# Two packed images out of one PSUM sum: one 32-bit integer pass in place of a rounding pass and a subtraction

## The chip, the cores and the metric

The kernel runs on one core of a Trainium2 chip. A core has five engines that run beside each other and meet at semaphores: TensorE (PE in the profile), VectorE (DVE), ScalarE (ACT), GpSimd (POOL) and SyncE (SP, which here only starts transfers). The metric is the device time of the whole kernel in microseconds. Before the change it was 318.55 us, the median of three runs (317.15 to 320.28).

## The reference, cut to what matters

A batch of 32 images with 64 channels of 28 x 28 passes through two blocks. The first one is the binary convolution block that the change touches:

```
xr  = tile(_gn(x), (1, 4, 1, 1))                   # 4 groups, all with the same input
out = conv3x3(sign(xr), sign(w1), groups=4)        # integers
out = relu(batchnorm(out, bn1))
out = conv3x3(sign(out), sign(w2), groups=4)       # sign of a relu: 0 or 1, "the gate"
out = batchnorm(out, bn2) * lambdas
out = sum over the 4 groups
x   = x + relu(out + _gn(x))
```

The second block multiplies the normalised x by a resized mask, computes a 7 x 7 attention convolution over three planes, multiplies by its sigmoid, normalises, scales, applies a relu and adds the result to x. In both blocks `_gn` is a normalisation over pairs of channels.

Because both convolutions take signs or gates, their sums are small integers. That allows two images to be computed in one sum: one image's value is multiplied by a large factor, the other's is added, and the two are taken apart afterwards.

## The kernel before

**Tiles.** The 32 images make 16 tiles (`NT`) of two images. A tile is 128 partitions (2 images x 64 channels) by 784 pixels. Tile t goes through the first block in iteration k = t of a software pipeline of 15 turns (k = 1 to 15, with a head for tile 0 and a tail), and through the steps of the second block in the iterations after it.

**First convolution.** `join` (L857) adds 2046 (`IMG`) times the first image's signs to the second image's signs, `pack_signs` (L439) copies the result to `E`, and `conv1` (L871) computes, for each of two halves q of the output channels, 784 sums of the form 2046*a + b. They lie in PSUM (`big`, in slots shared with other sums). ACT's `round_sums1` (L449) takes them out in two passes: L452 divides by 2046 and adds a large constant, which rounds to a, and L457 takes the constant away again and writes a as 16-bit floats in `first`. DVE's `gates` (L610) then has three instructions for each q: L612 compares a with a threshold and writes 1024 or 0 to `gate0`, L614 computes b = sum - 2046*a in PSUM, and L618 compares b, adds `gate0` and writes the packed gates to `S2`.

**Second convolution.** `conv2` (L884) runs over the two halves hh of the image rows, `round_sums2` (L459) and `move_back` (L467) on ACT and `split_sums` (L623) on DVE take the two images' sums apart into `RD`, `mix` (L898) sums the groups with weights `wa`, and `finish_block` (L630) on DVE adds the normalised x.

**Order.** Each engine has one instruction stream, written out by hand, and nothing is reordered. In turn k it is:

- PE: `conv1(k,0)`, `group_2(k-2)`, `conv1(k,1)`, `mix(k-1)`, `join(k+1)`, three `turn(k-2)`, `conv2(k,0)`, `conv2(k,1)`, and for odd k an `attention`.
- ACT: word or round of `c2(k-1,1)`, its move to `RD`, `sign_x(k+1)`, `round_sums1(k,0)`, `normalise2(k-2)`, `round_sums1(k,1)`, `relu_block(k-1)`, `pack_signs(k+1)`, `last_relu(k-5)`, the same for `c2(k,0)`, and for odd k a `sigmoid`.
- DVE: `split_sums(k-1,1)`, `terms2(k-2)` (four one-column instructions, L580 to L585), `stats_o(k-5)`, `gates(k,0)`, `finish_block(k-1)`, `gates(k,1)`, three `reduce_chunks(k-2)` (L651, L653), `stats_x(k+5)`, `split_sums(k,0)`, `stats_x1(k-1)`.
- POOL: `power2(k-2)`, `mask_column(k-2)`, `make_u(k-2)` (L349, 784 columns), `scale3(k-5)` (five one-column instructions, L374 to L382), `add_x(k-1)` (L367), `attend(k-4)` (L362), `last_sum(k-5)` (L387).

`turn(k-2,2)` on PE waits for the first of the three `reduce_chunks`, and stands ahead of `conv2(k,0)`. `group_2(k-2)` on PE waits for `stats_x1(k-2)` on DVE. `finish_block(k-1)` waits for `mix(k-1)`.

## Time and profile before

| | |
|---|---|
| median of the runs | 318.55 us (317.15 to 320.28) |
| span of the profiled execution, first to last instruction | 313.7 us |
| mean granted TensorE clock | 0.917 |
| PE busy | 239.8 us, 76% |
| DVE busy | 233.7 us, 74% |
| ACT busy | 184.0 us, 59% |
| POOL busy | 159.5 us, 51% |
| DMA | 28.86 MB, mean 92 GB/s |

The profiled execution's own time is not given apart from its span. The span leaves out what lies around the first and the last instruction: 318.55 - 313.7 = 4.85 us by the median.

A row of the timeline reads: start in us from the span's start, duration in us, engine, line, operation, what is written <- what is read, count, and in brackets the engine's idle time before it with what ended it. A row of the groups reads: line, engine, operation, tiles, shape and type, count | busy us in total, mean ns of one | idle us of the engine before them. In this profile the duration of one instruction overlaps the start of the next one on its engine by a little under 0.1 us when nothing separates them.

### The profile page before, as it was taken

The page shows a single profiled execution, that of the slowest core. Times are in us where ns is not written, and L with a number is a line of the kernel's source. Part 1 is how long each engine was busy: PE and PEld are TensorE (multiplying, and loading weights), DVE is VectorE, ACT ScalarE, POOL GpSimd, SP SyncE. Part 2 cuts the span into 40 slices and gives each one's busy share as a digit, 9 for nine tenths or more (in the row PEclk, how much of TensorE's full clock was granted, in tenths as well). Part 3 has the DMA queues.
Part 4 walks back from the last instruction along what each step waited for, and adds up shares of the span by engine and source line. Part 5 has one row for each costly group of instructions (what it writes and reads, how often), then busy time and mean ns, then how long its engine had stood idle before and what let it go on. Part 6 is the DMA issues. An engine that isn't in the chain of part 4 may idle for free.

```text
span 313.7 us, 7083 instructions
## 1 busy us (share of the span) xinstructions
PE 239.8 (76%) x2742; PEld 152.2 (49%) x2742; DVE 233.7 (74%) x554; ACT 184.0 (59%) x223; POOL 159.5 (51%) x215
## 2 busy tenths in 40 slices
PE   7294798687888778888887697969696969676860
PEld 3252555345554445445554464546454645454550
DVE  3338754769886896979998969899968687758373
ACT  3434252384858584848486848675876768544221
POOL 3200410222423456576747656774768475938763
PEclk9858677699999999979999999999999999979885
DMA  7980000523015402631253314211611141131113
GB/s 202 310 270 3 0 2 0 155 65 106 2 54 135 124 27 78 174 95 64 86 155 101 104 58 131 80 51 55 154 54 53 74 137 53 53 117 38 51 53 154
DMA packets 11946, 28.86 MB, mean 92 GB/s; under 512 B 2285, under 2 KB 3565, under 8 KB 11757
## 3 DMA queue, kind: packets, MB, share of 16 engines
q1 hardware_dynamic: 11481, 28.13, 29.2%
q8 instruction: 22, 0.36, 0.5%
q10 hardware_dynamic: 432, 0.29, 0.4%
q14 instruction: 11, 0.09, 0.1%
HBM read 21.79 MB, written 6.61 MB: 91 GB/s over the span
## 4 chain that ended last, share of the span: by engine, by line
PE 31%; DVE 28%; issue 17%; ACT 15%; DMA 3%; POOL 3%; SPq 0%; ACTq 0%; DVEq 0%; POOLq 0%
PE big L892 15%; DVE big L614 9%; ACT round L465 5%; PE small L938 5%; ACT first L457 3%; DVE bnst L556 3%; DMA X<-in_x 3%; PE small L927 3%; ACT round L452 3%; ACT signs L437 3%; DVE gate L612 3%; DVE red L651 2%; DVE RD L627 2%; DVE S L618 2%; PE big L878 2%
## 5 line engine op out<-in xcount | busy, mean ns | idle before, releaser
L892 PE MATMUL big<-S,w2t 64*64 64x392 f16 x1152 | 59.3, 361 | 7.5 <-DVE S L618 7.5
L465 ACT ACTIVATE round<-big 128x784 f16<-128x784 f32 x32 | 26.1, 815 | 54.7 <-PE big L892 54.7
L878 PE MATMUL big<-E,w1t 64*128 64x392 f16 x576 | 55.8, 337 | 0.0
L927 PE MATMUL small<-cs,o 128*112 128x130 f32 x224 | 32.9, 287 | 27.2 <-DVE red L653 24.1
L627 DVE SCALAR_TENSOR_TENSOR RD<-round,big 128x784 f16<-128x784 f16 x32 | 30.7, 960 | 25.6 <-ACT round L465 25.6
L892 PEld LDWEIGHTS big<-S,w2t 64*64 64x64 f16 x1152 | 34.9, 115 | 27.1 <-DVE S L618 4.3
L927 PEld LDWEIGHTS small<-cs,o 128*112 128x112 f32 x224 | 26.4, 176 | 35.3 <-DVE red L653 27.4
L349 POOL TENSOR_TENSOR o<-o,mask_b 128x784 f32<-128x784 f32 x16 | 29.5, 1845 | 21.9 <-ACT o L484 21.9
L909 PE MATMUL big<-RD,wa 128*64 128x392 f16 x384 | 38.2, 352 | 1.3 <-DVE RD L627 1.3
L341 POOL TENSOR_TENSOR r<-ve,mhalf 128x1 f32<-128x1 f32 x16 | 8.9, 559 | 56.0 <-DVE ve L585 56.0
L556 DVE BATCH_NORM_STATS2 bnst<-X 128x6 f32<-128x392 f32 x64 | 32.8, 554 | 5.3 <-DMA X<-in_x 5.3
L878 PEld LDWEIGHTS big<-E,w1t 64*128 64x128 f16 x576 | 25.9, 95 | 21.1 <-issue 5.0
L367 POOL TENSOR_TENSOR X<-X,acc 128x784 f32<-128x784 f32 x15 | 27.7, 1843 | 15.4 <-ACT acc L478 15.4
L618 DVE SCALAR_TENSOR_TENSOR S<-big,thr,gate 128x784 f16<-128x784 f32 x32 | 33.2, 1038 | 1.1
L614 DVE SCALAR_TENSOR_TENSOR big<-first,big 128x784 f32<-128x784 f16 x32 | 31.1, 972 | 0.0
L909 PEld LDWEIGHTS big<-RD,wa 128*64 128x64 bf16 x384 | 21.7, 116 | 16.1 <-issue 4.7
L452 ACT ACTIVATE round<-big 128x784 f32<-128x784 f32 x32 | 25.7, 804 | 5.9 <-PE big L878 5.8
L472 ACT ACTIVATE RD<-round 128x784 f16<-128x784 f16 x32 | 27.4, 857 | 1.0
L457 ACT ACTIVATE first<-round 128x784 f16<-128x784 f32 x32 | 27.4, 857 | 1.0
L478 ACT ACTIVATE acc<-acc,b 128x784 f32<-128x784 f32 x16 | 15.2, 948 | 20.4 <-DVE acc L635 20.4
L362 POOL TENSOR_TENSOR o<-o,att_b 128x784 f32<-128x784 f32 x14 | 25.9, 1852 | 0.0
L651 DVE TENSOR_REDUCE red<-small 112x6 f32<-112x384 f32 (+1 forms) x48 | 22.0, 463 | 4.6 <-PE small L927 4.1
(119 smaller groups left out, 355.5 us busy)
## 6 DMA issues: line engine op xcount, KB each, us to landing
X<-in_x SPq DMA_DIRECT2D x16, 392.0 KB, 6.4
mask_b<-mask_rows SPq DMA_DIRECT2D x32, 196.0 KB, 3.5
out<-o SPq DMA_DIRECT2D x16, 392.0 KB, 2.3
att_b<-attention_rows SPq DMA_DIRECT2D x28, 196.0 KB, 3.9
o<-in_w SPq DMA_DIRECT2D x3, 576.0 KB, 9.7
o<-in_masks SPq DMA_DIRECT2D x1, 512.0 KB, 11.0
cs<-in_cst SPq DMA_DIRECT2D x1, 385.0 KB, 11.1
o<-in_sel SPq DMA_DIRECT2D x1, 343.0 KB
```

The costliest lines, as they stand in the source:

```text
L349: pool.tensor_tensor(o[:, t, :], o[:, t, :], mask_b[:, t % 2, :], ALU.mult).then_inc(u_ready, 1)
L452: act.activation(round1[:, :], sums(f"c1_{q}"), ACT.Copy, bias=ROUND, scale=1.0 / IMG)\
L457: act.activation(first[:, q, :], round1[:, :], ACT.Copy, bias=-ROUND).then_inc(whole1, 1)
L465: act.activation(round2[:, hh, :], sums(f"c2_{hh}"), ACT.Copy, bias=BASE - MID).then_inc(rounded2, 1)
L556: dve.bn_stats(bnst[:, n, t, i, :], src[:, HALF * i:HALF * (i + 1)]).then_inc(stats[n], 1)
L614: dve.scalar_tensor_tensor(sums(f"c1_{q}"), first[:, q, :], -IMG, sums(f"c1_{q}"), ALU.mult, ALU.add)\
L618: dve.scalar_tensor_tensor(inside(S2[:, t % 2, q, :]), sums(f"c1_{q}").rearrange("p (h w) -> p h w", w=W), thr[:, q:q + 1], gate0[:, q, :] ...
L627: dve.scalar_tensor_tensor(RD[:, t % 2, hh, 1, :], round2[:, hh, :], BASE, sums(f"c2_{hh}"), ALU.subtract, ALU.subtract).then_inc(split, 1)
L878: mm = pe.matmul(acc[:, LOW + HALF * hh:LOW + HALF * (hh + 1)], w1t[64 * hh:64 * hh + 64, s, q * P:(q + 1) * P], window(RH * hh, s // 3, s ...
L892: mm = pe.matmul(acc[64 * q:64 * q + 64, LOW + HALF * r:LOW + HALF * (r + 1)], w2t[64 * r:64 * r + 64, s, 64 * q:64 * q + 64], window(RH * ...
L909: mm = pe.matmul(big[SLOT["y"]][64 * i:64 * i + 64, at:at + HALF], wa[:, i, r, n, :], RD[:, t % 2, hh, i, HALF * r:HALF * (r + 1)], start= ...
L927: mm = pe.matmul(small[1 - n % 2][0:CP, at:at + P + 2], o[:, t, CP * j:CP * (j + 1)], cs[:, K_ID:K_ID + P + 2], start=True, stop=True)
```

## The change

For the first convolution ACT makes one pass over each packed sum. It multiplies by 65536/2046, adds 32768 and writes a 32-bit integer (`word1`). The upper 16 bits of that integer are a and the lower 16 bits are proportional to b plus an offset. DVE reads both through 16-bit views of the same memory (`high1`, `low1`), in which neighbouring elements are four bytes apart. The second pass of ACT (L457) and DVE's subtraction in PSUM (L614) are gone. The last gate instruction reads `low1` from SBUF where it read PSUM, and a second threshold `thr_low` in the new scale is computed once in the head.

For the second convolution ACT writes `word2` in 32 bits. The first image's value is copied from `high2` by ACT, with as many passes as before. `split_sums` becomes a one-input instruction on `low2` where it was a two-input one on `round2` and PSUM. `wa` loses its factor -1024.

Two waits move: `join(t)` and `conv1(t,1)` on PE wait for ACT's integer pass, where they waited for DVE's gates and split.

```diff
-        round1 = sb("round1", [P, HW], F32)
-        first = sb("first", [P, 2, HW], F16)
-        round2 = sb("round2", [P, 2, HW], F16)
+        word1 = sb("word1", [P, 2, HW], I32)
+        word2 = sb("word2", [P, 2, HW], I32)
...
+        low1, high1 = (word1[:, :, :].bitcast(dt).rearrange("p q (n two) -> p q n two", two=2)[:, :, :, h]
+                       for h, dt in ((0, U16), (1, I16)))
...
-            def round_sums1(t, q):
+            def words1(t, q):
                 act.wait_ge(conv1_done, t * 2 + q + 1)
-                wait(act, whole1, t * 2 + q)
-                act.activation(round1[:, :], sums(f"c1_{q}"), ACT.Copy, bias=ROUND, scale=1.0 / IMG)\
-                   .then_inc(rounded1, 1)
-                act.wait_ge(rounded1, t * 2 + q + 1)
-                wait(act, parted1, t * 2 + q - 1)
-                wait(act, gated0, t * 2 + q - 1)
-                act.activation(first[:, q, :], round1[:, :], ACT.Copy, bias=-ROUND).then_inc(whole1, 1)
+                wait(act, gated, t * 2 + q - 1)
+                act.activation(word1[:, q, :], sums(f"c1_{q}"), ACT.Copy, bias=WORD / 2, scale=WORD / IMG)\
+                   .then_inc(worded1, 1)
...
-                act.activation(round2[:, hh, :], sums(f"c2_{hh}"), ACT.Copy, bias=BASE - MID).then_inc(rounded2, 1)
+                act.activation(word2[:, hh, :], sums(f"c2_{hh}"), ACT.Copy, bias=LIFT, scale=WORD)\
+                   .then_inc(worded2, 1)
...
-                act.activation(RD[:, t % 2, hh, 0, :], round2[:, hh, :], ACT.Copy, bias=-BASE).then_inc(whole2, 1)
+                act.activation(RD[:, t % 2, hh, 0, :], high2[:, hh, :], ACT.Copy).then_inc(whole2, 1)
...
             def gates(t, q):
-                dve.wait_ge(whole1, t * 2 + q + 1)
-                dve.tensor_scalar(gate0[:, q, :], first[:, q, :], thr[:, q:q + 1], GATE, ALU.is_gt, ALU.mult)\
+                dve.wait_ge(worded1, t * 2 + q + 1)
+                dve.tensor_scalar(gate0[:, q, :], high1[:, q, :], thr[:, q:q + 1], GATE, ALU.is_gt, ALU.mult)\
                    .then_inc(gated0, 1)
-                dve.scalar_tensor_tensor(sums(f"c1_{q}"), first[:, q, :], -IMG, sums(f"c1_{q}"), ALU.mult, ALU.add)\
-                   .then_inc(parted1, 1)
-                dve.wait_ge(parted1, t * 2 + q + 1)
+                if t == 0:
+                    dve.wait_ge(thr_ready, 1)
+                dve.wait_ge(gated0, t * 2 + q + 1)
                 wait(dve, conv2_done, t * 2 - 2)
                 dve.scalar_tensor_tensor(inside(S2[:, t % 2, q, :]),
-                                         sums(f"c1_{q}").rearrange("p (h w) -> p h w", w=W), thr[:, q:q + 1],
+                                         low1[:, q, :].rearrange("p (h w) -> p h w", w=W), thr_low[:, q:q + 1],
                                          gate0[:, q, :].rearrange("p (h w) -> p h w", w=W), ALU.is_gt, ALU.add)\
                    .then_inc(gated, 1)
...
-                    dve.scalar_tensor_tensor(RD[:, t % 2, hh, 1, :], round2[:, hh, :], BASE, sums(f"c2_{hh}"),
-                                             ALU.subtract, ALU.subtract).then_inc(split, 1)
+                    dve.tensor_scalar(RD[:, t % 2, hh, 1, :], low2[:, hh, :], LIFT, 1.0 / UNIT,
+                                      ALU.subtract, ALU.mult).then_inc(split, 1)
...
-                wait(pe, gated, 2 * t - 1)
+                wait(pe, worded1, 2 * t - 1)
...
-                    wait(pe, split, 2 * t - 1)
+                    wait(pe, worded2, 2 * t - 1)
```

DVE's stream in an iteration of the loop before, from the second `gates` over the three `reduce_chunks` and `stats_x` to `split_sums(k,0)`; the names behind the arrow are what is read (`first` is a, `big` is PSUM):

```order
L614 SCALAR_TENSOR_TENSOR big<-first,big 128x784
L618 SCALAR_TENSOR_TENSOR S<-big,thr,gate 128x28x28 [waits conv2_done,parted1]
L651 TENSOR_REDUCE red<-small 112x3x2 [waits att_done,turned]
...
L558 BN_AGGR mv<-bnst 128x2 [waits stats0]
L627 SCALAR_TENSOR_TENSOR RD<-round,big 128x784 [waits y_done,rounded2]
```

The same place after the change, where `word` is one of the two integer tiles in SBUF:

```order
L619 TENSOR_SCALAR gate<-word,thr 128x784 [waits worded1]
L625 SCALAR_TENSOR_TENSOR S<-word,thr_low,gate 128x28x28 [waits conv2_done,gated0]
L658 TENSOR_REDUCE red<-small 112x3x2 [waits att_done,turned]
...
L565 BN_AGGR mv<-bnst 128x2 [waits stats0]
L634 TENSOR_SCALAR RD<-word 128x784 [waits y_done,worded2]
```

Nothing has changed its place; the 784-column subtraction is out, the gate instruction reads two tiles of SBUF and no PSUM, and the split reads one tile of SBUF. ACT's stream in an iteration before, from the move of `c2(k-1,1)` to the first convolution's second half:

```order
L472 ACTIVATE RD<-round 128x784 [waits y_done,rounded2]
L437 ACTIVATE signs<-X,nm 128x784 [waits joined,mean1]
L452 ACTIVATE round<-big 128x784 [waits whole1,conv1_done]
L457 ACTIVATE first<-round 128x784 [waits gated0,parted1,rounded1]
L484 ACTIVATE o<-X,nmr,r 128x784 [waits shift2]
L452 ACTIVATE round<-big 128x784 [waits whole1,conv1_done]
L457 ACTIVATE first<-round 128x784 [waits gated0,parted1,rounded1]
```

and after it:

```order
L479 ACTIVATE RD<-word 128x784 [waits y_done,worded2]
L447 ACTIVATE signs<-X,nm 128x784 [waits joined,mean1]
L462 ACTIVATE word<-big 128x784 [waits gated,conv1_done]
L491 ACTIVATE o<-X,nmr,r 128x784 [waits shift2]
L462 ACTIVATE word<-big 128x784 [waits gated,conv1_done]
```

Two of the seven rows are out, so `normalise2` (`o<-X,nmr,r`) stands right behind the first integer pass.

## Rows read from the trace of the kernel before

**Rows 1.** The page: the span, and busy time by engine (us, share of the span).
```profile
span 313.7 us, 7083 instructions
...
PE 239.8 (76%) x2742; PEld 152.2 (49%) x2742; DVE 233.7 (74%) x554; ACT 184.0 (59%) x223; POOL 159.5 (51%) x215
```

**Rows 2.** Instruction groups (shapes apart): total us, mean ns | idle before.
```profile
L614 DVE SCALAR_TENSOR_TENSOR big<-first,big 128x784 f32<-128x784 f16 x32 | 31.1, 972 | 0.0
...
L618 DVE SCALAR_TENSOR_TENSOR S<-big,thr,gate 128x784 f16<-128x784 f32 x32 | 33.2, 1038 | 1.1
...
L627 DVE SCALAR_TENSOR_TENSOR RD<-round,big 128x784 f16<-128x784 f16 x32 | 30.7, 960 | 25.6 <-ACT round L465 25.6
...
L612 DVE TENSOR_SCALAR gate<-first,thr 128x784 f16<-128x784 f16 x32 | 13.4, 419 | 14.0 <-ACT first L457 13.9
...
L457 ACT ACTIVATE first<-round 128x784 f16<-128x784 f32 x32 | 27.4, 857 | 1.0
...
L580 DVE TENSOR_SCALAR nm<-small 128x1 f32<-128x1 f32 x18 | 2.8, 155 | 1.6 <-PE small L845 0.8 <-PE small L854 0.7
```

**Rows 3.** Timeline, tile 8 to 9: start us, us, engine line op, tiles, [idle before].
```profile
168.81 0.82 ACT L465 ACTIVATE round<-big 128x784 f16<-128x784 f32 x1 [2.44 <-PE big L892]
...
171.75 0.93 DVE L627 SCALAR_TENSOR_TENSOR RD<-round,big 128x784 f16<-128x784 f16 x1
...
171.88 0.38 PE L854 MATMUL small<-mv,cs 128*128 128x2 f32 x2
...
172.87 0.80 ACT L452 ACTIVATE round<-big 128x784 f32<-128x784 f32 x1
...
173.83 2.18 PE L909 MATMUL big<-RD,wa 128*64 128x392 f16 x24
...
174.59 0.43 DVE L612 TENSOR_SCALAR gate<-first,thr 128x784 f16<-128x784 f16 x1 [0.28 <-ACT first L457]
...
175.57 1.84 POOL L349 TENSOR_TENSOR o<-o,mask_b 128x784 f32<-128x784 f32 x1 [1.38 <-ACT o L484]
...
176.89 1.02 DVE L635 SCALAR_TENSOR_TENSOR acc<-X,r,big 128x784 f32<-128x784 f32 x1
...
177.83 0.42 DVE L612 TENSOR_SCALAR gate<-first,thr 128x784 f16<-128x784 f16 x1
...
180.12 0.55 DVE L651 TENSOR_REDUCE red<-small 112x6 f32<-112x384 f32 x1
...
182.97 0.82 ACT L465 ACTIVATE round<-big 128x784 f16<-128x784 f32 x1 [2.44 <-PE big L892]
...
182.99 1.85 POOL L387 TENSOR_TENSOR o<-o,X 128x784 f32<-128x784 f32 x1
```

**Rows 4.** Timeline, tile 9 to 10, a stretch with an attention.
```profile
186.48 0.80 ACT L465 ACTIVATE round<-big 128x784 f16<-128x784 f32 x1
...
190.64 0.42 DVE L612 TENSOR_SCALAR gate<-first,thr 128x784 f16<-128x784 f16 x1 [0.64 <-ACT first L457]
...
191.62 1.84 POOL L349 TENSOR_TENSOR o<-o,mask_b 128x784 f32<-128x784 f32 x1 [1.75 <-ACT o L484]
...
196.16 0.55 DVE L651 TENSOR_REDUCE red<-small 112x6 f32<-112x384 f32 x1
```

**Rows 5.** Timeline at two places where DVE and POOL overlap.
```profile
152.79 1.85 POOL L387 TENSOR_TENSOR o<-o,X 128x784 f32<-128x784 f32 x1
...
152.88 1.78 DVE L608 TENSOR_SCALAR b<-nmr,beta 128x4 f32<-128x4 f32 x1
...
285.02 1.85 POOL L362 TENSOR_TENSOR o<-o,att_b 128x784 f32<-128x784 f32 x1
...
285.55 2.15 DVE L641 TENSOR_TENSOR X<-X,acc 128x784 f32<-128x784 f32 x1
...
286.82 2.57 POOL L387 TENSOR_TENSOR o<-o,X 128x784 f32<-128x784 f32 x1
```

**Rows 6.** Timeline, the first gates of the program.
```profile
24.64 0.42 DVE L612 TENSOR_SCALAR gate<-first,thr 128x784 f16<-128x784 f16 x1 [4.03 <-ACT first L457]
```

49 lines of the change are left out of this document (29 added, 20 removed).

## The prediction

> **What bounds the kernel now.** I read the page first, then the groups of instructions, then the timeline of two stretches of the loop. The page shows no full engine: PE is busy for 76% and DVE for 74% of the span [rows 1]. So the bound is a loop through several engines. The timeline of one turn, from the first L465 of tile 8 to that of tile 9, takes 182.97 - 168.81 = 14.16 us [rows 3]. I call its start T. ACT takes the sums out (L465, two halves), makes the next signs, and rounds conv1's first half (L452, L457). DVE had waited only 0.28 us when the first gate instruction L612 started at T+5.78. Three gate instructions bring it to `finish_block` at T+8.08 (L635), and three more, from 177.83 on, to the first `reduce_chunks` at 180.12: that is 2.29 us for one `gates`. PE's last `turn` waits for that reduce, and `conv2` stands behind it, so the next T follows 182.97 - 180.12 = 2.85 us after the reduce. PE does not bind the first half of the turn: `mix` had ended at 173.83 + 2.18 = 176.01, 0.88 us before `finish_block` began. A turn with an attention (T to T longer by PE's attention work) has the same chain behind its second L465 at 186.48, there with 0.64 us of waiting for L457 [rows 4]. Both `gates` of a turn lie on the chain, and that makes DVE's subtraction L614 (972 ns, 32 times, no idle time before it) the heaviest thing that the change removes [rows 2].
>
> **What the change removes and adds.**
>
> *The gates.* Out: L614. The last instruction of `gates` keeps its operation; I give it its present 1.04 us [rows 2]. All 784-column instructions of DVE with two inputs lie within 0.96 to 1.04 us whether they read PSUM twice or once, so I see no gain from leaving PSUM. The first one, L612, costs 0.42 us now on dense 16-bit data; in the new kernel its input stands in every second 16-bit place. Bounds: 0.42 below, and above the full-rate 0.96 of L627 [rows 2]. One column costs 0.155 us (L580), so the 784 dense columns take 0.26 us more than one. If only one value comes with each 4-byte word, that part doubles: 0.155 + 0.53 = 0.69 us. I take 0.69. A `gates` then lasts 0.69 + 0.04 (the second waits for the first) + 0.95 (1.04 less the overlap with the next instruction) = 1.68 us, which is 0.61 less than 2.29.
>
> *ACT.* The second pass L457 goes (0.86 us, 32 times) [rows 2]. The one pass writes 4 bytes as L452 did, so it stays at 0.80. Bounds of the integer output and of the copy from every second place: nothing, and the 0.06 between 0.80 and 0.86 us. ACT has 41% of the span idle [rows 1], which hides that.
>
> *The splits.* One input in place of two; the same 0.69 instead of 0.96: 0.27 us less each, bounds 0.42 and 0.96.
>
> *Without anything in the way* the first `gates` of a turn could start about 0.9 us earlier, and then `finish_block` meets a new bound: it cannot start before `mix` has ended, 176.01 + 0.07 = 176.08, in place of 176.89. So 0.81 us are won before it and 0.61 behind it, 1.42 us per turn.
>
> *The port.* Two places of the trace say that this is not what will happen. L641, a DVE instruction with two inputs in SBUF, began 0.53 us after POOL's L362, lasted 2.15 us, and POOL's next instruction L387, which started with DVE waiting, lasted 2.57 us instead of 1.85 [rows 5]. DVE waited for POOL to end, then POOL waited for DVE. L608, a one-input instruction of four columns with input and output in SBUF, lasted 1.78 us and ended with POOL's L387 at 154.66 [rows 5]; one column of such an operation costs 0.155 us. By these rows a DVE instruction with two SBUF inputs, or one SBUF input and an SBUF output in this fast form, and a POOL instruction exclude each other, and who comes first keeps the way to his end. Before the change only L612 was of that kind, and it sat in gaps of POOL. Now all six big instructions of a turn are: two L612, two last gates, two splits; against POOL's four 1.84 us instructions.
>
> The Trainium skill says the same in *SBUF — State Buffer*, section "Who interferes with whom": VectorE and GpSimd share a port pair that is locked for a whole instruction, by VectorE instructions with two SBUF inputs and by copies and tensor_scalar in the two-port modes. It speaks against this change: without that rule the sum would be 1.42 us per turn, with it what follows.
>
> *A turn with an attention* [rows 4]. L612 starts 0.64 us earlier, at 190.00; the last gate runs from 190.73 to 191.77. `make_u` (L349, 191.62 before) is wanted about 0.7 us earlier, at 190.9, since the removed L457 stood before its ACT source; it is blocked until 191.77 and ends 1.84 later, at 193.61. The second L612 would be wanted 0.94 after `finish_block`, near 193.0, and waits for 193.61. The reduce comes at 193.61 + 1.68 = 195.29 instead of 196.16: 0.87 us won.
>
> *A turn without an attention* [rows 3]. The end of `make_u` again starts the second gates, so the next T comes 1.68 + 2.85 = 4.53 us after that end, and `make_u` starts 6.37 before T. `last_sum` (L387) follows the start of `make_u` by 182.99 - 175.57 = 7.42 us, so it starts at T+1.05, or up to 1.2 later if DVE holds up POOL's small instructions (0.69 + 1.04, less what overlaps). The first split is wanted at T+0.86 and waits until T+1.05 or T+2.25, where the instruction before `last_sum` ends. The second one (T+2.94 before) then waits for the end of `last_sum`, near T+3.5 or T+4.75. From there 0.61 (the split, less overlap) and 1.72 (what stood between L627 at 171.75 and L612 at 174.59, less L627's own 0.84 and the 0.28 idle) lead to the first gates, at T+5.8 or T+7.1. PE's `group_2` (L854, T+3.07) is held only in the second case, by 1.05. Then 0.73 + 1.04 for the gates, 1.84 for `make_u` behind them and 4.53 to the next T: 14.0 or 15.2 us, against 14.16. I take the middle, 0.43 us lost.
>
> *Head and tail.* The first gates waited 4.03 us for ACT [rows 6]; they start 0.86 earlier, and both `gates` of tile 0 are 0.61 shorter: 2.08 us. Tile 1 gives 0.61. The tail gives one split, 0.27. In the turns from tile 1 to 2 and 2 to 3 POOL has neither `attend` nor `last_sum` yet; there only the wait for `make_u` is left, some 1.1 us won each.
>
> *Sum*: -2.08 - 0.61 - 2 x 1.1 - 6 x 0.87 + 6 x 0.43 - 0.27 = -7.8 us. Of the profiled execution's span of 313.7 us that leaves 305.9; with the 4.85 us by which the median lies above that span, 310.7. I say 310.5.
>
> **The rivals.**
>
> *A, the port does not matter.* DVE and POOL fall beside each other, or the new forms do not need the shared way. Then 14 turns at 1.42 and 2.96 from head, tile 1 and tail: -22.8 us, 295.7. For it: L612 and POOL lived side by side for the whole loop. Against it: rows 5.
>
> *B, reading every second place runs at full rate* (0.96 us) and then needs no port in the one-input forms. A `gates` saves 0.34, the splits nothing, and only the last gate meets `make_u`. An attention turn then wins about 0.8, another between 1.1 won and 0.7 lost: 305 to 313.
>
> *C, slower: `make_u` overtakes the first gates.* In my timetable the last gate instruction of the first half starts at 190.73 and `make_u` is wanted at 190.9. Once the first gate instruction takes over 0.2 us longer than I say, or POOL comes that much earlier, POOL goes first and the last gate waits 1.84 us. `finish_block` stands behind it on DVE, and PE behind that. An attention turn then costs 0.15 more than before, another one about 1.3 more, and the first two win nothing: -2.96 + 6 x 0.15 + 6 x 1.3 = +5.7 us, 324.3.
>
> *D, the change does nothing.* Each turn without attention loses what the other wins (15.2 us each, +1.05 instead of +0.43): 310.7 + 6 x 0.62 = 314.4, near the edge.
>
> **How the numbers follow.** 1% of 318.55 is 3.2 us, about what a measurement of this kernel can tell from no change; faster means under 315.4. My forecast with D as its upper end (304 to 318) 0.52; A 0.20; B 0.15; C 0.13. Faster: all of A, nearly all of B, and about 0.4 of the 0.52, 0.73. Same: the rest of the forecast and a little of B and C, 0.15. Slower: 0.12. The range takes A's value at its lower end and stops short of C: 296 to 320; the forecast's own range is 304 to 318.
>
> **What would show each step right or wrong.** The first gate instruction at 0.69 us where POOL is idle, the last at 1.04, the split at 0.69. The price of the port: maxima near 2 to 3 us in these three groups, starts of POOL's L349 at the end of a gate, and POOL's 1.84 us instructions and its one-column ones getting longer. Attention turns shorter by about 0.9 us and the others unchanged. If the three groups all show a median equal to their minimum, A is right. If `finish_block` starts right behind `mix` in every turn, PE has become the bound. If the last gate of the first half regularly lasts near 2.9 us, C is right. The forecast is wrong above all if POOL's phase in the turn is another than I worked out, since each of its four big instructions is longer than any gap I reasoned with.

## The result and the profile after the change

The changed kernel takes 302.33 us (median of 298.91 to 304.31) against 318.41 us for the kernel before on the same chip; the ratio is 0.9445 with a 95% interval of 0.9385 to 0.9505. The medians are of all executions; every ratio and interval here is taken from those alone that ran undisturbed, since some executions take about a per cent longer at a lower granted clock, and so 0.9445 isn't 302.33/318.41. A second measurement beside later experiments gave 300.9 us, ratio 0.9475 (0.9425 to 0.9526). So the change wins 16 to 18 us. I had forecast 8, and a range of 296 to 320: the sign was right, the time lay inside the range, and the size was half of what came. The profiled execution has a span of 297.1 us beside 313.7 before.

The page after the change, its span and its busy times (before: [rows 1]):

```profile
span 297.1 us, 6991 instructions
...
PE 238.0 (80%) x2742; PEld 152.4 (51%) x2742; DVE 216.5 (73%) x523; ACT 159.2 (54%) x191; POOL 182.9 (62%) x215
```

DVE is busy 17 us less, ACT 25 us less, and POOL is busy 23 us *more*, although it has the same 215 instructions. The groups show why (line engine, tiles, count | busy us, mean ns | idle before; before: [rows 2]):

```profile
L634 DVE TENSOR_SCALAR RD<-word 128x784 f16<-128x784 uint16 x32 | 33.1, 1035 | 22.2 <-ACT word L471 22.2
...
L625 DVE SCALAR_TENSOR_TENSOR S<-word,thr_low,gate 128x784 f16<-128x784 uint16 x32 | 34.7, 1084 | 1.3
...
L619 DVE TENSOR_SCALAR gate<-word,thr 128x784 f16<-128x784 int16 x32 | 22.8, 712 | 6.1 <-ACT word L462 6.1
...
L359 POOL TENSOR_TENSOR o<-o,mask_b 128x784 f32<-128x784 f32 x16 | 35.6, 2226 | 15.4 <-ACT o L491 15.4
...
L397 POOL TENSOR_TENSOR o<-o,X 128x784 f32<-128x784 f32 x13 | 28.3, 2180 | 0.0
...
L386 POOL TENSOR_TENSOR r<-ve,mhalf 128x1 f32<-128x1 f32 x16 | 18.3, 1141 | 1.3
```

`make_u` (L359) has a mean of 2226 ns and `last_sum` (L397) of 2180 where POOL's instructions of this size took 1.84 and 1.85 us before [rows 3], and the one-column power L386 doubled to 1141 ns. The DVE split L634 has a mean of 1035 ns. The means hide two populations; the split and the gate by line (duration min/median/max):

```profile
L619 DVE TENSOR_SCALAR gate<-word,thr x32: 574/627/1280, 22.2 to 251.0; 128x784 f16<-128x784 int16 x32
```
```profile
L625 DVE SCALAR_TENSOR_TENSOR S<-word,thr_low,gate x32: 1036/1040/2497, 23.0 to 252.1; 128x784 f16<-128x784 uint16 x32
```
```profile
L634 DVE TENSOR_SCALAR RD<-word x32: 514/571/1894, 36.7 to 260.3; 128x784 f16<-128x784 uint16 x32
```

Free of POOL, the strided gate instruction takes 0.574 to 0.63 us and the split 0.51 to 0.57; the last gate takes the 1.04 us it took from PSUM. The maxima are waits for POOL.

The timeline of a turn without attention (start, us, engine line, tiles, [idle before]; before: [rows 3]):

```profile
155.77 0.82 ACT L471 ACTIVATE word<-big 128x784 int32<-128x784 f32 x1 [0.24 <-PE big L901]
156.24 1.85 POOL L372 TENSOR_TENSOR o<-o,att_b 128x784 f32<-128x784 f32 x1
...
156.62 1.89 DVE L634 TENSOR_SCALAR RD<-word 128x784 f16<-128x784 uint16 x1 [0.98 <-ACT word L471]
...
158.06 2.16 POOL L397 TENSOR_TENSOR o<-o,X 128x784 f32<-128x784 f32 x1
...
159.62 1.02 DVE L634 TENSOR_SCALAR RD<-word 128x784 f16<-128x784 uint16 x1
...
162.20 0.58 DVE L619 TENSOR_SCALAR gate<-word,thr 128x784 f16<-128x784 int16 x1
162.81 1.04 DVE L625 SCALAR_TENSOR_TENSOR S<-word,thr_low,gate 128x784 f16<-128x784 uint16 x1
...
163.17 2.38 POOL L359 TENSOR_TENSOR o<-o,mask_b 128x784 f32<-128x784 f32 x1 [1.01 <-ACT o L491]
...
164.88 1.09 DVE L619 TENSOR_SCALAR gate<-word,thr 128x784 f16<-128x784 int16 x1
...
169.82 0.83 ACT L471 ACTIVATE word<-big 128x784 int32<-128x784 f32 x1 [0.23 <-PE big L901]
```

The turn lasts 169.82 - 155.77 = 14.05 us, 0.11 less than the 14.16 before. The first split (156.62) waits for `attend` (L372), and `last_sum` (L397) then waits for the split; the second split (159.62) waits for `last_sum`; `make_u` (L359) starts 0.36 us behind the last gate L625, is held by it, and holds the second first-gate instruction (164.88) in turn. The next turn has an attention (before: [rows 4]):

```profile
173.33 0.80 ACT L471 ACTIVATE word<-big 128x784 int32<-128x784 f32 x1
...
177.37 1.04 DVE L625 SCALAR_TENSOR_TENSOR S<-word,thr_low,gate 128x784 f16<-128x784 uint16 x1
...
177.72 2.38 POOL L359 TENSOR_TENSOR o<-o,mask_b 128x784 f32<-128x784 f32 x1 [1.01 <-ACT o L491]
...
180.70 1.33 POOL L386 TENSOR_TENSOR r<-ve,mhalf 128x1 f32<-128x1 f32 x1
...
181.52 0.55 DVE L658 TENSOR_REDUCE red<-small 112x6 f32<-112x384 f32 x1
```

From the second L471 at 173.33 to the reduce at 181.52 it takes 8.19 us, against 196.16 - 186.48 = 9.68 before.

Lengths of the turns from tile to tile, measured from one first L465 (after: L471) to the next, in the profiled executions (us). The last four columns are experiments, told below; in "POOL cut" POOL's large instructions are shortened to 8 columns:

| turn | before | after | last gate from PSUM (e5) | first half only (e8) | before, POOL cut (e7) | after, POOL cut (e6) |
|---|---|---|---|---|---|---|
| 0 to 1 | 24.57 | 25.21 | 25.99 | 28.09 | 27.35 | 26.26 |
| 1 to 2 | 15.48 | 14.05 | 13.87 | 13.43 | 15.28 | 13.95 |
| 2 to 3 | 14.17 | 12.94 | 12.94 | 15.36 | 14.16 | 12.95 |
| 3 to 4, attention | 16.04 | 14.47 | 14.46 | 14.47 | 16.05 | 14.46 |
| 4 to 5 | 14.17 | 12.72 | 12.62 | 13.05 | 14.16 | 12.63 |
| 5 to 6, attention | 17.26 | 14.57 | 14.46 | 14.56 | 17.48 | 14.46 |
| 6 to 7 | 14.51 | 14.32 | 13.05 | 14.41 | 14.35 | 12.95 |
| 7 to 8, attention | 16.05 | 14.57 | 14.62 | 14.57 | 16.04 | 14.46 |
| 8 to 9 | 14.16 | 14.05 | 12.63 | 13.04 | 14.17 | 12.63 |
| 9 to 10, attention | 16.05 | 14.56 | 14.45 | 14.56 | 16.05 | 14.46 |
| 10 to 11 | 14.35 | 14.34 | 13.06 | 15.30 | 14.35 | 12.95 |
| 14 to 15 | 13.77 | 14.04 | 12.62 | 13.04 | 13.88 | 12.63 |

The gain of the change is in the turns with an attention, 1.5 us each, and in the early ones. The turns without attention from tile 6 to tile 13 win 0.0 to 0.2 us, and the one from tile 14 to 15 loses 0.27.

One length is the same in all these profiles: the next turn starts 2.85 or 2.86 us after the first `reduce_chunks` of the turn, as long as TensorE's granted clock stays at 1.00 (2.4 GHz). Where it fell to 0.50 (1.2 GHz) behind an idle time of PE, it took 3.54 to 4.45 us. In the kernel before that happened once, from tile 5 to 6 (4.07 us), and in the changed one never between tile 1 and tile 15. So 1.2 of the 2.7 us won in that turn belong to the clock in this one profile, and not to the chain.

### The profile page after: what moved, and what is told of

Same layout as the page of the kernel before. It is cut to its first block, busy times and chain, and to the rows that moved or that the text cites. A ratio compares the mean times of both kernels' runs of the same rounds, so it can differ in the third digit from the quotient of the medians.

```text
span 297.1 us, 6991 instructions
## 1 busy us (share of the span) xinstructions
PE 238.0 (80%) x2742; PEld 152.4 (51%) x2742; DVE 216.5 (73%) x523; ACT 159.2 (54%) x191; POOL 182.9 (62%) x215
## 4 chain that ended last, share of the span: by engine, by line
PE 56%; DVE 23%; issue 11%; DMA 3%; ACT 3%; POOL 3%; SPq 1%; POOLq 0%; DVEq 0%; ACTq 0%
PE big L901 16%; PE big L887 13%; PE big L918 10%; DVE gate L619 5%; PE small L947 5%; PE small L936 4%; DVE RD L634 4%; DVE bnst L563 4%; DMA X<-in_x 3%; DVE S L625 2%; PE small L991 2%; ACT word L471 2%; DVE red L658 2%; PE small L863 1%; POOL o L359 1%
## 5 line engine op out<-in xcount | busy, mean ns | idle before, releaser
L936 PE MATMUL small<-cs,o 128*112 128x130 f32 x224 | 35.1, 303 | 26.6 <-POOL o L359 19.3
L634 DVE TENSOR_SCALAR RD<-word 128x784 f16<-128x784 uint16 x32 | 33.1, 1035 | 22.2 <-ACT word L471 22.2
L936 PEld LDWEIGHTS small<-cs,o 128*112 128x112 f32 x224 | 28.8, 190 | 35.7 <-POOL o L359 25.2
L359 POOL TENSOR_TENSOR o<-o,mask_b 128x784 f32<-128x784 f32 x16 | 35.6, 2226 | 15.4 <-ACT o L491 15.4
L471 ACT ACTIVATE word<-big 128x784 int32<-128x784 f32 x32 | 26.1, 815 | 27.1 <-PE big L901 27.1
L377 POOL TENSOR_TENSOR X<-X,acc 128x784 f32<-128x784 f32 x15 | 29.3, 1957 | 13.9 <-ACT acc L485 13.9
L625 DVE SCALAR_TENSOR_TENSOR S<-word,thr_low,gate 128x784 f16<-128x784 uint16 x32 | 34.7, 1084 | 1.3
L507 ACT ACTIVATE o<-o,bi,sc 128x784 f32<-128x784 f32 x16 | 16.7, 1042 | 33.4 <-POOL sc L392 33.4
L485 ACT ACTIVATE acc<-acc,b 128x784 f32<-128x784 f32 x16 | 15.2, 949 | 26.8 <-DVE acc L642 26.8
L462 ACT ACTIVATE word<-big 128x784 int32<-128x784 f32 x32 | 25.8, 806 | 6.5 <-PE big L887 6.3
L397 POOL TENSOR_TENSOR o<-o,X 128x784 f32<-128x784 f32 x13 | 28.3, 2180 | 0.0
L918 PEld LDWEIGHTS big<-RD,wa 128*64 128x64 bf16 x384 | 20.8, 112 | 14.3 <-issue 4.7
L479 ACT ACTIVATE RD<-word 128x784 f16<-128x784 int16 x32 | 27.4, 857 | 1.0
L619 DVE TENSOR_SCALAR gate<-word,thr 128x784 f16<-128x784 int16 x32 | 22.8, 712 | 6.1 <-ACT word L462 6.1
```

Source lines behind the costliest of these rows:

```text
L359: pool.tensor_tensor(o[:, t, :], o[:, t, :], mask_b[:, t % 2, :], ALU.mult).then_inc(u_ready, 1)
L377: pool.tensor_tensor(X[:, t, :], X[:, t, :], acc0[:, t % 2, :], ALU.add).then_inc(x1_ready, 1)
L397: pool.tensor_tensor(o[:, t, :], o[:, t, :], X[:, t, :], ALU.add).then_inc(fin_added, 1)
L471: act.activation(word2[:, hh, :], sums(f"c2_{hh}"), ACT.Copy, bias=LIFT, scale=WORD)\
L619: dve.tensor_scalar(gate0[:, q, :], high1[:, q, :], thr[:, q:q + 1], GATE, ALU.is_gt, ALU.mult)\
L625: dve.scalar_tensor_tensor(inside(S2[:, t % 2, q, :]), low1[:, q, :].rearrange("p (h w) -> p h w", w=W), thr_low[:, q:q + 1], gate0[:, q, ...
```

## The experiments

The theory is that of the prediction: the changed kernel's chain is much shorter, and a part of what it wins is given back because DVE's and POOL's large instructions now exclude each other. The rivals are that the port costs nothing, and, for the gain itself, that ACT's second pass rather than DVE's subtraction carried it.

**e1 and e8, the first convolution's half alone.** The second convolution keeps its 16-bit tile and its split with one input in SBUF and one in PSUM.

```diff
-                act.activation(word2[:, hh, :], sums(f"c2_{hh}"), ACT.Copy, bias=LIFT, scale=WORD)\
+                act.activation(round2[:, hh, :], sums(f"c2_{hh}"), ACT.Copy, bias=BASE - MID)\
...
-                    dve.tensor_scalar(RD[:, t % 2, hh, 1, :], low2[:, hh, :], LIFT, 1.0 / UNIT,
-                                      ALU.subtract, ALU.mult).then_inc(split, 1)
+                    dve.scalar_tensor_tensor(RD[:, t % 2, hh, 1, :], round2[:, hh, :], BASE, sums(f"c2_{hh}"),
+                                             ALU.subtract, ALU.subtract).then_inc(split, 1)
```

> Only the first convolution's half of the change; the second convolution keeps its 16-bit tile and the split that reads SBUF and PSUM (0.96 us, no second SBUF operand). Port theory (a DVE instruction with two SBUF inputs, or in the fast one-input form, and a POOL instruction exclude each other): the first split of a turn no longer waits for POOL's attend (1.88 us in the changed kernel, 0.97 here), group_2 and mix on PE come about 0.9 us earlier, turns without attention are 0.5 to 0.9 us shorter, so 296 to 299 us. Rival (the port costs nothing, only busy time counts): the split is 0.39 us longer than the free 0.57, so 303 to 306 us.

> The first convolution's half alone once more, for a profile at full clock (the first one was taken at the low clock throughout). Port theory: the first split of a turn lasts 0.97 us and does not wait for POOL; group_2 is no longer held; turns without attention under 13.8 us, with attention near 14.6. If turns without attention stay at 14.0 to 14.3, the split was not what held them and another wait took its place.

Measured: e1 304.74 us, ratio 0.9576 (0.9493 to 0.9659), e8 303.47 us, ratio 0.9561 (0.9484 to 0.9637). Both totals lie in the range that I had given the rival (303 to 306 us), not in that of the port theory (296 to 299), so the totals alone speak against it. The profile of e1 was taken in an execution in which TensorE was granted 0.555 of its clock on average, near the low of its two levels (span 394.2 us); e8 exists for that reason. A turn without attention of e8:

```profile
162.45 0.82 ACT L471 ACTIVATE round<-big 128x784 f16<-128x784 f32 x1 [0.24 <-PE big L901]
162.90 1.86 POOL L372 TENSOR_TENSOR o<-o,att_b 128x784 f32<-128x784 f32 x1
...
163.30 0.97 DVE L634 SCALAR_TENSOR_TENSOR RD<-round,big 128x784 f16<-128x784 f16 x1 [0.98 <-ACT round L471]
...
167.87 0.57 DVE L619 TENSOR_SCALAR gate<-word,thr 128x784 f16<-128x784 int16 x1
...
175.49 0.82 ACT L471 ACTIVATE round<-big 128x784 f16<-128x784 f32 x1 [0.24 <-PE big L901]
```

The split (163.30) starts inside `attend` (162.90) and is not held, the first gates come 5.42 us after the turn's start instead of 6.43, and the turn lasts 13.04 us instead of 14.05. That part of the theory holds (0.97 us, under 13.8 us), and yet the whole kernel is not faster than the changed one. The table shows where it went: the turns 2 to 3 and 10 to 11 are 2.4 and 1.0 us longer. In the first of them POOL's `add_x` overtook the last gate:

```profile
85.65 2.13 POOL L377 TENSOR_TENSOR X<-X,acc 128x784 f32<-128x784 f32 x1
...
86.12 2.51 DVE L625 SCALAR_TENSOR_TENSOR S<-word,thr_low,gate 128x784 f16<-128x784 uint16 x1
```

`add_x` (L377) began 0.47 us before L625, which then lasted 2.51 us instead of 1.04. The other one, 10 to 11, has no such meeting. There PE was idle for 2.26 us behind `make_u`, its clock fell to 0.50, and the next turn came 3.76 us after the reduce instead of 2.86:

```profile
200.23 3.03 PE L936 MATMUL small<-cs,o 128*112 128x130 f32 x14 [2.26 <-POOL o L359]
203.19 3.63 PE L901 MATMUL big<-S,w2t 64*64 64x392 f16 x72
```

In the changed kernel the same 72 matmuls take 3.25 us. An idle time of PE of the same 2.26 us in the turn from 6 to 7 of e8 was followed by no fall of the clock; why one was and the other not stays open. From the start of tile 1's turn to that of tile 15, e8 takes 197.95 us, the changed kernel 197.81 and the same kernel in e9 197.11. What the split won in the late turns (1.0 us each in three of them) went into one meeting of the same two engines, one fall of the clock, and 0.1 to 0.3 us in each of two other turns. Most of the rest of the difference is the head (0 to 1, 28.09 against 25.21), but the changed kernel itself took 27.80 us there in e9, see the last section.

**e2, the second convolution's half alone.** The first one keeps ACT's two passes and the subtraction.

```diff
-                    dve.scalar_tensor_tensor(RD[:, t % 2, hh, 1, :], round2[:, hh, :], BASE, sums(f"c2_{hh}"),
-                                             ALU.subtract, ALU.subtract).then_inc(split, 1)
+                    dve.tensor_scalar(RD[:, t % 2, hh, 1, :], low2[:, hh, :], LIFT, 1.0 / UNIT,
+                                      ALU.subtract, ALU.mult).then_inc(split, 1)
```

> Only the second convolution's half; the first one keeps ACT's two passes and DVE's subtraction in PSUM. Port theory: the first split starts while POOL's last_sum runs and lasts near 1.5 us instead of 0.97, the second one 0.57; what one loses the other wins, 317 to 321 us. Rival (only busy time counts): both splits 0.39 us shorter, the 0.28 us of waiting before the first gates grow, 314 to 317 us.

Measured: 317.99 us, ratio 0.9932 (0.9862 to 1.0002); the turns are the old ones, 14.16 and 16.05. The first split starts inside POOL's `last_sum` and waits for it, the second one is free:

```profile
182.88 1.86 POOL L396 TENSOR_TENSOR o<-o,X 128x784 f32<-128x784 f32 x1
...
183.71 1.46 DVE L636 TENSOR_SCALAR RD<-word 128x784 f16<-128x784 uint16 x1 [0.98 <-ACT word L474]
...
187.19 0.57 DVE L636 TENSOR_SCALAR RD<-word 128x784 f16<-128x784 uint16 x1 [0.84 <-ACT word L474]
```

1.46 us against 0.97 before, then 0.57: the forecast "near 1.5, then 0.57" was met. The total can't tell the theory from its rival, since the interval reaches from 1.4% faster to no change; the turns and these two rows can. The second half of the change is worth nothing that I can tell from zero by itself.

**e3, ACT's second pass put back** into the changed kernel.

```diff
+                act.wait_ge(worded1, t * 2 + q + 1)
+                act.activation(first[:, q, :], high1[:, q, :], ACT.Copy).then_inc(whole1, 1)
...
-                dve.wait_ge(worded1, t * 2 + q + 1)
-                dve.tensor_scalar(gate0[:, q, :], high1[:, q, :], thr[:, q:q + 1], GATE, ALU.is_gt, ALU.mult)\
+                dve.wait_ge(whole1, t * 2 + q + 1)
+                dve.tensor_scalar(gate0[:, q, :], first[:, q, :], thr[:, q:q + 1], GATE, ALU.is_gt, ALU.mult)\
```

> The changed kernel with ACT's second pass put back (it copies the upper half to a dense 16-bit tile that the first gate instruction reads at 0.42 us). If ACT's pass was on the chain everywhere, 14 turns at 0.86 us and the head: 313 to 316 us. By the timeline of the changed kernel it is on the chain only in turns with an attention (the first gates wait there for ACT, elsewhere for DVE's own work): about +0.6 in each of six or seven of those turns, +0.7 in the head: 305 to 308 us.

Measured: 304.25 us, ratio 0.9575 (0.9465 to 0.9686). Attention turns take 14.93 us, 0.36 more than without the pass, and the other late ones 13.63 to 13.92, 0.4 *less*, because the gate instruction on the dense tile takes 0.37 to 0.43 us instead of 0.57. In an attention turn the first gates wait for ACT:

```profile
181.27 0.43 DVE L622 TENSOR_SCALAR gate<-first,thr 128x784 f16<-128x784 f16 x1 [0.64 <-ACT first L466]
```

I had expected +0.6 in an attention turn and 305 to 308 us, which was a little too much. So ACT's 27 us of second passes were worth the 1.9 to 3.4 us between 304.25 and the two medians of the changed kernel, and a part of that is one odd turn of 16.62 us (3 to 4) in which POOL held the last gate:

```profile
97.65 2.71 DVE L628 SCALAR_TENSOR_TENSOR S<-word,thr_low,gate 128x784 f16<-128x784 uint16 x1
97.69 1.84 POOL L378 TENSOR_TENSOR X<-X,acc 128x784 f32<-128x784 f32 x1 [0.29 <-ACT acc L488]
```

The gate's recorded start is 0.04 us ahead of POOL's, and it lost all the same, so recorded starts that close don't say who wins. The rival "ACT's pass carried the gain" (313 to 316) is out.

**e4, a DVE pass over PSUM put back** between the two gate instructions.

```diff
+                dve.scalar_tensor_tensor(sums(f"c1_{q}"), gate0_old[:, q, :], -IMG, sums(f"c1_{q}"), ALU.mult, ALU.add)\
+                   .then_inc(parted1, 1)
...
-                wait(pe, worded1, 2 * t - 1)
+                wait(pe, gated, 2 * t - 1)
```

> The changed kernel with a 784-column DVE instruction between SBUF and PSUM put back into each gates (0.97 us, its result unused), join waits for the gates again. If the subtraction was simply on the chain, +1.0 us at the second gates and part of that at the first: 302 + 14 x 1.0 to 1.6 = 316 to 325 us. If in addition POOL's make_u now starts before the last gate of the first half and holds it 1.84 us (rival C of the prediction), 325 to 335 us, and that instruction's median is near 2.5 us in the first half.

Measured: 365.82 us, ratio 1.1513 (1.1441 to 1.1584). That is 47 us slower than the kernel *before*, which has the same DVE passes and one more on ACT, and 31 us above the worst I had expected. The turns take 18.4 to 19.1 us. The profile shows what I had called rival C:

```profile
236.96 1.85 POOL L361 TENSOR_TENSOR o<-o,mask_b 128x784 f32<-128x784 f32 x1 [1.01 <-ACT o L493]
237.58 2.07 DVE L630 SCALAR_TENSOR_TENSOR S<-word,thr_low,gate 128x784 f16<-128x784 uint16 x1
...
241.65 1.84 POOL L379 TENSOR_TENSOR X<-X,acc 128x784 f32<-128x784 f32 x1
242.10 2.22 DVE L630 SCALAR_TENSOR_TENSOR S<-word,thr_low,gate 128x784 f16<-128x784 uint16 x1
...
244.91 0.78 PE L942 MATMUL small<-cs,o 128*112 128x130 f32 x2 [3.30 <-DVE red L665]
```

With 0.97 us more between the two gate instructions, POOL's `make_u` (236.96) starts 0.62 us ahead of the last gate (L630, 237.58), which lasts 2.07 us. In the second gates `add_x` (241.65) does the same, 2.22 us. Each turn thus pays 1.9 us for the two passes and 2.2 us for the two lost races, less some 1.3 us of waits for POOL that the changed kernel had and e4 has not: in the turn from 8 to 9 the reduce comes 13.99 us after the start instead of 11.19. A third part is the clock. PE stands idle for 3.30 us (244.91), and its granted clock is 0.50 from 245 to 248 us; the next turn starts 3.65 to 4.45 us after the reduce instead of 2.86. That happens in every one of the 14 turns and makes 18.2 of the 61.8 us by which this loop is longer (259.6 against 197.8 from tile 1 to 15). My 325 to 335 had one lost race per turn and no clock in it. So e4 shows the race, but it doesn't price the subtraction by itself. The margin by which the changed kernel wins that race is 0.36 us (162.81 to 163.17).

**e5, the last gate without a second SBUF operand.** It reads the packed sum from PSUM and so leaves out the right comparison of the second image.

```diff
-                                         low1[:, q, :].rearrange("p (h w) -> p h w", w=W), thr_low[:, q:q + 1],
+                                         sums(f"c1_{q}").rearrange("p (h w) -> p h w", w=W), thr_low[:, q:q + 1],
...
-                wait(pe, worded1, 2 * t - 1)
+                wait(pe, gated, 2 * t - 1)
```

> The changed kernel, but the last gate instruction reads the packed sum in PSUM instead of the lower half in SBUF, so that it has one SBUF tensor (join waits for the gates again, since PSUM is read longer). It leaves out the right comparison of the second image. Port theory: POOL's make_u lasts 1.85 instead of 2.38 us, POOL's one-column power in scale3 0.57 instead of 1.33, attend and last_sum end about 1.3 us earlier, the first split waits less in turns without attention (0.5 to 0.8 us each) and the second gates wait 0.15 less in the others: 294 to 299 us beside about 302 for the changed kernel. Rival (these waits are hidden): 301 to 303 us.

Measured: 293.23 us, ratio 0.9237 (0.9162 to 0.9311): 8 to 9 us under the changed kernel, and 0.8 under the range that I had given.

```profile
175.92 1.04 DVE L625 SCALAR_TENSOR_TENSOR S<-big,thr_low,gate 128x784 f16<-128x784 f32 x1
...
176.28 1.85 POOL L359 TENSOR_TENSOR o<-o,mask_b 128x784 f32<-128x784 f32 x1 [1.01 <-ACT o L491]
```
```profile
L625 DVE SCALAR_TENSOR_TENSOR S<-big,thr_low,gate x32: 1036/1037/1041, 23.8 to 246.2; 128x784 f16<-128x784 f32 x32
```

The instruction has the same 1.037 us with one operand in PSUM, but POOL's `make_u` beside it now takes 1.85 us, and no instance of L625 lasts longer than 1.041 us. The turns fall to 12.62 to 13.06 and 14.46 us.

**e6 and e7, POOL's large instructions cut to 8 columns** in the kernel after and before. Both leave out most of the mask and attention products and of two sums.

```diff
-                    pool.tensor_tensor(o[:, t, :], o[:, t, :], mask_b[:, t % 2, :], ALU.mult).then_inc(u_ready, 1)
+                    pool.tensor_tensor(o[:, t, 0:8], o[:, t, 0:8], mask_b[:, t % 2, 0:8], ALU.mult).then_inc(u_ready, 1)
```

> The changed kernel with POOL's four large instructions cut from 784 to 8 columns (it leaves out most of mask product, attention product and two sums); DVE's instructions then never wait for POOL. If the port takes gain away, this is well under the changed kernel by more than the next run is under the kernel before: 12.7 to 13.2 us per turn without attention and 14.4 with, 289 to 294 us. If the port costs nothing: 299 to 302 us.

> The kernel before with the same cut of POOL's instructions. In its turns POOL stands on no chain, so 14.2 and 16.05 us per turn stay and only the tail, where make_u, attend and the last sums are in series with other work, gets shorter by about 5 us: 311 to 314 us. The difference to the run with the changed kernel is what the change is worth without the port: 20 to 23 us if rival A of the prediction was priced right.

Measured: 287.23 us (ratio 0.9038, 0.8965 to 0.9111) and 314.57 us (0.9874, 0.9744 to 1.0004). Without POOL's large instructions the change is worth 27.3 us; with them it is 16.1 (302.33 against 318.41). From tile 1 on, the turns of e7 are those of the kernel before within 0.2 us, save two with a fall of TensorE's clock (17.48 from 5 to 6, 17.24 from 13 to 14), so POOL stood on no chain of the loop there. Both totals missed what I had expected, e6 by 1.8 us below and e7 by 0.6 above. From tile 1 on, the turns of e6 are those of e5 within 0.11 us, save one of 14.62 in e5. In the loop, from tile 1 to tile 15, the kernel before takes 212.3 us, the changed one 197.8, e5 190.3 and e6 190.1: the port costs the changed kernel 7.7 us there, and taking the last gate off it gives all but 0.2 back.

**e9, e10, e11 and e12, looking for a faster version.** e9 is the changed kernel once more. The other three try to sort the meetings by order. e10 is the first half alone with two edits:

```diff
                     pool.wait_ge(block_relu, t + 1)
+                    pool.wait_ge(gated, 2 * t + 4)
...
+                if k in (3, 7, 11):
+                    make_bias1(batch(k + 1))
                 gates(k, 0)
```

e11 is the whole change with the same edits; e12 is e10 with `make_bias1` moved behind `finish_block`:

```diff
                 finish_block(k - 1)
+                if k in (3, 7, 11):
+                    make_bias1(batch(k + 1))
```

> The changed kernel itself, beside the next two on one chip. If the times of its first measurement (298.9 to 304.3) are the spread of TensorE's granted clock in the head and tail, it stays at 299 to 304 us with the same turns of the loop (14.0 and 14.6 us).

> Only the first convolution's half of the change, and two orders changed: POOL's add_x waits until the last gate of its turn is done (in the profile of e8 it went first at 56.4 and 85.65 and held that gate for 1.46 us), and DVE makes the bias terms of the batches (L613, L615) before the first gates instead of behind the reduces (where L615 waited 1.6 us for POOL). Port theory: tile 1 and turns 2 to 3, 6 to 7 and 10 to 11 get 1.5 to 2.3 us shorter each: 296 to 299 us, faster than the changed kernel. Rival (these waits are hidden by other work): 303 to 305 us as in e1 and e8.

> The whole change with the same two orders. Tile 1 gets 1.46 us shorter and turn 10 to 11 about 0.3: 299 to 301 us. Turns without attention stay at 14.0 us since the first split still waits for attend.

> Only the first convolution's half of the change, POOL's add_x behind the last gate of its turn, and the bias terms of a batch between finish_block and the second gates instead of behind the reduces (e10 had them before the first gates, where they let POOL's make_u go first and hold the gate for 2.67 us). There the port is POOL's anyway. Port theory: no turn above 14.6 us, turns without attention 13.0 to 13.5 us, 293 to 298 us. Rival (the loop's waits only move): 300 to 304 us.

Measured: e9 300.9 us (0.9475), e10 306.51 us with executions scattered from 298.72 to 308.48, so that it decides nothing, e11 300.79 us (0.9504, 0.9458 to 0.955), e12 301.65 us (0.951, 0.9459 to 0.9561). None beats the changed kernel clearly. The totals of e9 and e11 are as expected; e10 was expected at 296 to 299 and e12 at 293 to 298, and both missed. The wait of `add_x` did in tile 1 what it should; the gate that lasted 2.50 us there has its 1.04 in e11, where POOL now comes behind:

```profile
51.91 2.12 POOL L377 TENSOR_TENSOR X<-X,acc 128x784 f32<-128x784 f32 x1 [10.79 <-ACT acc L485]
52.38 2.50 DVE L625 SCALAR_TENSOR_TENSOR S<-word,thr_low,gate 128x784 f16<-128x784 uint16 x1
```
```profile
52.51 1.04 DVE L626 SCALAR_TENSOR_TENSOR S<-word,thr_low,gate 128x784 f16<-128x784 uint16 x1
...
53.69 1.84 POOL L378 TENSOR_TENSOR X<-X,acc 128x784 f32<-128x784 f32 x1 [12.44 <-DVE S L626]
```

But turns 6 to 7 and 10 to 11 got longer, 15.86 and 15.57 us in e11 and 17.19 and 15.72 in e10. In e10, 0.3 us of bias terms ahead of the first gates were enough to let `make_u` go level with the last gate, in both turns:

```profile
139.19 0.23 DVE L616 TENSOR_SCALAR b<-nmr,beta 128x4 f32<-128x4 f32 x1
...
139.99 2.67 DVE L626 SCALAR_TENSOR_TENSOR S<-word,thr_low,gate 128x784 f16<-128x784 uint16 x1
139.99 1.84 POOL L359 TENSOR_TENSOR o<-o,mask_b 128x784 f32<-128x784 f32 x1 [1.01 <-ACT o L492]
```

In e11 no last gate is held (its longest is 1.043 us). There the clock is the larger part: PE was idle for 1.89 us before its `turn` matmuls, its clock fell to 0.50 in both turns, and the next turn came 4.05 and 3.62 us after the reduce instead of 2.86. Behind `finish_block` (e12) the same turns take 15.50 and 15.67 us, no last gate is held either, and the clock fell in both (3.54 and 3.73 us). The turn from 6 to 7 of e10 has such a fall too. I had not looked for this in the expectations. My expectation for e12, no turn above 14.6 us, failed, and I leave the best place for these small instructions open. The version that would be worth having is one with the timing of e5 and a right second comparison; I found no form of it.

## Why the prediction was right or wrong, point by point

**What bounds the kernel, and what the change removes: right.** With POOL out of the way (e7 to e6) an attention turn gets 1.59 us shorter and a late one without attention 1.3 to 1.5, and in e3 ACT's pass costs 0.36 us of an attention turn, net of what the dense gate instructions give back. e8 has the old split and the same 14.56 us in an attention turn, so the new split gives nothing there. What is left of the 1.5 us is DVE's subtraction and the two moved waits of PE; no run takes out the subtraction alone. Leaving PSUM made the last gate no faster (1.04 us). ACT's integer pass kept 0.80 us (L462 median 0.803), its strided copy 0.857.

**The port: right in kind.** First split behind `attend`, second behind `last_sum`, `make_u` behind the last gate, the second gates behind `make_u`: all four meetings are in the timeline of the changed kernel where the prediction put them, and e5, e6 and e7 show that removing them gives the time back. The trace agrees with what the Trainium skill states in *SBUF — State Buffer*, section "Who interferes with whom", on which instructions contend: the strided split and the last gate with two SBUF inputs are held, the one with an input in PSUM (e5) is not. The page says that the pair is locked for the whole instruction; how the recorded times look at its end comes next.

**The step that failed: the price of a turn with the port.** The attention turn was to win 0.87 us and won 1.48 to 1.57 (the one from tile 5 to 6 won 2.69, because it had taken 17.26 us before, in a stretch with a fall of TensorE's clock). The turn without attention was to lose 0.43 and won 0.0 to 0.2 from tile 6 to 13, lost 0.27 from 14 to 15, and won 1.45 from tile 4 to 5. Three parts of that error can be read from the rows. First, the strided one-input instruction takes 0.57 us where I had doubled the column part of L612 to 0.69; it runs free once on the path of each turn (162.20). Second, I let the waiting instruction start its full duration at the recorded end of the one that held the port. In the rows `make_u` ends 1.70 us after the gate that held it (163.17 + 2.38 against 162.81 + 1.04) where I had 1.84, and the gate instruction held by `make_u` ends 0.42 us after it (164.88 + 1.09 against 165.55), the held first split 0.42 us after `attend`, where I had 0.69. So a held instruction ends as if it had started some 0.15 us before the recorded end of its holder; whether the port is free that early or the held one has a start-up of its own that needs no port, no run here tells. My own [rows 5] had this already: L387 ended at 289.39, 1.69 us and not 1.85 behind the L641 that had held it (287.70), and the four-column L608, 0.23 us when free, ended 0.02 us behind L387. Third, these add up along the chain: in the turn without attention my second case had the first gates at T+7.1, the end of `make_u` at T+10.7 and the next T at 15.2; measured are T+6.43, T+9.78 and 14.05. POOL's phase was that of this second case, `attend` ending at T+2.3 (T+2.25 in the prediction). With the measured sizes the same timetable, worked through again after the result, gives T+6.43, T+9.78 and 14.04 for this turn, 0.12 us won, and 1.40 won for the attention turn. The sum is then -14.3 us instead of -7.8, or 304.3 us.

Two things in the loop stay outside that. The timetable put `last_sum` into all six turns, but in the one from tile 4 to 5 POOL has none yet and `attend` ends at T+0.75, before the split is wanted at T+0.86; so it is an early turn like the first two, and wins 1.45. And 1.2 of the 2.69 us from 5 to 6 are the clock of the one profile before: luck, by which the gain looks that much larger in the spans of the two profiles.

In the sum: the six attention turns gave 10.2 us instead of 5.2, the six others from tile 4 on gave 1.6 instead of costing 2.6. These two terms are 9.2 us off, against 8.8 between the forecast 7.8 and the 16.6 by which the spans differ; the others nearly cancel (head 1.6 and the two first turns 0.5 better than forecast, tile 1 1.3 and the tail 1.1 worse).

**The head** gave 3.64 us up to the first L471 instead of 2.08. Part of that is scatter: the same point comes at 32.92, 33.92 and 33.04 us in three profiles with the whole change (after, e9, e11), and at 36.56 in the one before. Tile 1 was to give 0.61 and cost 0.64, because `add_x` took the port before its last gate (51.91, above). The prediction had no such meeting in it; e11 takes it away. The tail, from tile 15's first L471 to the end, was to give 0.27 and got 0.9 us longer; I haven't traced why.

**Rival A** was priced at 22.8 us and measured at 27.3 by e6 and e7, 23.3 of them in the loop, of which 2.6 are the two turns of e7 with a fall of the clock. That leaves 20.7 beside the 19.9 of its 14 turns, so the chain without the port was sized well. **Rival B** is out: the strided instruction takes 0.57 us and not 0.96. **Rival C** did not happen as a rule, but its mechanism is real and near: e4 pays it twice in each turn, e10 in two turns, and `add_x` does the same to one last gate in the changed kernel (tile 1), e3 and e8 have two such gates each. **Rival D** did not happen: the late turns without attention are about as long as before, but the others won more than it has to set off against them.

**The chances.** I gave the likeliest case an inner range of 304 to 318 us, and the median came at 302.33, 1.7 below it. The two errors in the turn without attention had opposite signs: the middle of two cases for POOL's phase was 0.62 us cheaper than the second case, which came, and the full durations made that second case 1.2 us too dear. In the attention turn only the second error was there, and nothing set it off. That the total still fell inside the outer range is owed to rival A's value at its lower end, not to the sum.

## What to carry to other kernels

Moving a DVE operand from PSUM to SBUF, or replacing a two-input instruction that reads PSUM by a fast one-input instruction on SBUF, can bring DVE into conflict with POOL where there was none. Count for each such instruction the POOL instructions of the turn and who starts first, since 0.3 us decide between nothing and 1.5 us. Look at what the wait does to TensorE's clock as well: in e4, e8, e11 and e12 PE stood idle for 1.9 to 3.3 us in some turns, and where the clock fell behind it, that cost up to 1.6 us more. When a shorter chain is forecast, check what the removed work was worth in each kind of turn: here the same edit won 1.5 us in one kind and 0.1 in the other. Where two engines exclude each other, take the second one's end from a pair of rows in which one holds the other, not from its full duration: here it was 0.15 us less each time, several times in a row on the chain.

## What the runs showed of the hardware that was not expected

POOL's one-column power is held as well: L386 has a median of 0.57 us in the kernel before and 0.58 in e5, whose last gates read PSUM, and of 1.33 us in the changed kernel, where it starts during a last gate. By the medians a DVE instruction of 784 columns thus costs POOL 0.76 us in a step that moves a single column.

Part of the scatter of the totals lies in TensorE's clock in the head, where PE is idle in between. The stretch from 30 to 40 us (columns: stretch, length, busy time of PE, PEld, DVE, ACT, POOL with the number of instructions, granted clock, DMA share, GB/s) and in it the 28 small matmuls of `band_matrices` (L991), first in the changed kernel:

```profile
30.00:40.00 10.00, 10.00 (x110) 7.02 (x104) 6.09 (x29) 2.76 (x4) 3.52 (x12) 0.67 0.01 2
```
```profile
33.32 3.06 PE L991 MATMUL small<-atw,o 28*112 28x36 f32 x28
```

and in e8:

```profile
30.00:40.00 10.00, 8.70 (x66) 7.29 (x66) 6.73 (x26) 1.68 (x2) 3.70 (x12) 0.50 0.00 0
```
```profile
34.90 5.43 PE L991 MATMUL small<-atw,o 28*112 28x36 f32 x28
```

In e8 the clock stayed at the low level, 0.50 or 1.2 GHz, through the whole stretch, and PE was idle for 1.3 us of it; in the changed kernel, where PE had no idle time from 30 us on, it rose as these matmuls began. They took 5.43 us in the one and 3.06 in the other, which is 2.4 of the 2.9 us by which the first turn of e8 is longer. I don't know whether that belongs to e8 or to the execution: in e9, the changed kernel once more, the same stretch was granted 0.50 too. This is as large as most differences between the variants, so they were compared by the turns of the loop, and not by the totals alone. There the granted clock is 0.99 to 1.00 on average from 100 to 260 us in the kernel before, the changed one and e8, and a single fall shows as a turn whose end comes late after its reduce.
